# A recurrent layer and a mixture of experts on one core: three transpositions go from TensorE to the DMA queue of SyncE

## What is computed

```python
def cell(h, x):                       # 256 steps, one after the other; D = 512
    gi, gh = x @ W_ih + b_ih, h @ W_hh + b_hh
    r = sigmoid(gi_r + gh_r); z = sigmoid(gi_z + gh_z)
    n = tanh(gi_n + r * gh_n)
    return (1 - z) * n + z * h
...
scores = einsum('btd,ed->bte', h, Wg)            # E = 8
probs  = softmax(top 2 of scores)
y = sum over the two experts e:  prob_e * ((silu(h @ W1[e].T) * (h @ W2[e].T)) @ W3[e].T)
out = x + y
```

## Time and profile before

| | |
|---|---|
| median of 3 runs | 1501.19 us |
| span of the profiled execution | 1501.1 us, 88729 instructions |
| time of the profiled execution outside its span | about 0.1 us, by the median of the runs |
| busy: PE, PEld | 1409.4 us (94%), 1227.2 us (82%) |
| busy: DVE, ACT, POOL | 1043.8 (70%), 896.3 (60%), 415.8 (28%) |
| ACT copies out of tr_ps and gn_bank | 56.3 (L845), 52.6 (L853), 9.0 and 10.0 (L856), 32.0 us (L863) |
| granted TensorE clock, mean | 0.976 |
| steps 52 to 255 of the recurrence | about 296 to 1356 us |
| the 20 tiles behind it | from about 1357 us |

### The profile page before, as it was taken

One profiled execution on the slowest core, in us unless ns is written; L12 is line 12 of the kernel. 1 busy time (PEld: TensorE's weight loads), 2 busy tenths in 40 slices (PEclk: granted clock), 3 DMA queues, 4 the chain that ended last, 5 costly groups with the idle time before them and its releaser, 6 DMA issues.

```text
span 1501.1 us, 88729 instructions
## 1 busy us (share of the span) xinstructions
PE 1409.4 (94%) x37804; PEld 1227.2 (82%) x37804; DVE 1043.8 (70%) x4116; ACT 896.3 (60%) x2319; POOL 415.8 (28%) x850
## 2 busy tenths in 40 slices
PE   2888878899999999999999999999999999998997
PEld 1888778888888888888888888888888888885664
DVE  7788887777677677777777767776777776764333
ACT  6677675555565556655556555665556655555664
POOL 1011112123322232222332223222333222326443
PEclk9999887899999999999999999999999999999999
DMA  8445413112221222212222122211222212223431
GB/s 290 124 130 140 134 45 90 40 32 40 46 39 39 46 46 40 39 39 46 40 46 40 39 46 46 41 38 40 46 40 46 40 39 47 39 40 79 60 49 16
DMA packets 99011, 88.64 MB, mean 59 GB/s; under 512 B 41407, under 2 KB 74175, under 8 KB 98624
## 3 DMA queue, kind: packets, MB, share of 16 engines
q0 software_dynamic: 17952, 33.64, 12.9%
q1 hardware_dynamic: 80672, 49.32, 11.5%
HBM read 59.12 MB, written 35.72 MB: 63 GB/s over the span
## 4 chain that ended last, share of the span: by engine, by line
PE 83%; DVE 10%; issue 3%; ACT 1%; POOL 1%; DMA 1%; SPq 0%; DVEq 0%; POOLq 0%; ACTq 0%
PE gn_bank L1366 12%; PE gz_ps L1366 12%; PE y_ps L1458 9%; PE b_ps L1388 9%; PE a_ps L1422 8%; PE b_ps L1422 8%; PE gi_ps L1388 8%; PE gr_ps L1357 6%; PE gr_ps L1351 6%; DVE wexp L1037 2%; PE tr_ps L1436 2%; PE tr_ps L1446 2%; PE tr_ps L1478 1%; DVE npre L1067 1%; DVE nmh L1073 1%
## 5 line engine op out<-in xcount | busy, mean ns | idle before, releaser
L1366 PE MATMUL gz_ps<-hlog,whh 128*128 128x32 f16 x8192 | 246.0, 177 | 6.1 <-issue 6.0
L1366 PE MATMUL gn_bank<-hlog,whh 128*128 128x32 f16 x8192 | 245.2, 177 | 2.4 <-issue 2.2
L625 POOL DMA_INDIRECT out_y<-work,mt x57 | 93.9, 1648 | 546.2 <-PE gz_ps L1366 309.6
L1366 PEld LDWEIGHTS gz_ps<-hlog,whh 128*128 128x128 f16 x8192 | 224.1, 96 | 6.9 <-issue 6.7
L1366 PEld LDWEIGHTS gn_bank<-hlog,whh 128*128 128x128 f16 x8192 | 224.2, 96 | 2.7 <-issue 2.7
L1351 PEld LDWEIGHTS gr_ps<-hlog,whh 128*128 128x128 f16 x4096 | 130.6, 96 | 53.9 <-DVE hlog L1080 32.4
L1351 PE MATMUL gr_ps<-hlog,whh 128*128 128x16 f16 x4096 | 141.9, 170 | 31.3 <-DVE hlog L1080 28.3
L1388 PE MATMUL b_ps<-xs,wih 128*128 128x64 f16 x4752 | 162.3, 197 | 3.4 <-issue 2.1
L1458 PE MATMUL y_ps<-wexp,work 128*128 x639 | 159.0, 382 | 1.9 <-ACT work L845 1.9
L1388 PEld LDWEIGHTS b_ps<-xs,wih 128*128 128x128 f16 x4752 | 153.3, 101 | 5.1 <-issue 3.5
L810 ACT ACTIVATE rs<-rpre,sc 128x64 f32<-128x64 f32 x256 | 88.0, 344 | 112.7 <-DVE rpre L1054 112.5
(11 more groups left out here) (217 smaller groups left out, 2550.3 us busy)
## 6 DMA issues: line engine op xcount, KB each, us to landing
wexp<-in_w_units SPq DMA_DIRECT2D x46, 256.0 KB, 3.8
x_raw<-in_x_feat SPq DMA_DIRECT2D x32, 256.0 KB, 3.7
out_y<-in_x_tok SPq DMA_DIRECT2D x16, 512.0 KB
h_tok<-xrow SPq DMA_DIRECT2D x32, 256.0 KB, 2.0
wexp<-in_w_hh SPq DMA_DIRECT2D x4, 768.0 KB, 6.8
wexp<-in_w_inproj SPq DMA_DIRECT2D x4, 768.0 KB, 11.8
wexp<-in_w_units SPq DMA_DIRECT2D x15, 192.0 KB, 4.5
mt<-meta SPq DMA_DIRECT2D x71, 1.0 KB, 1.7
```

Source lines behind the costliest of these rows:

```text
L625: pool.indirect_dma_start(out=out, out_offset=bass.IndirectOffsetOnAxis(ap=mt[:, j % RING, 0:1].bitcast(I32), axis=0), in_=ysc[y_slot(j)], ...
L1366: mm = pe.matmul(dst[:, j], whh[:, i, k, m * P:(m + 1) * P], h[:, k], start=False, stop=True, skip_group_check=True)
```

## The change

The three turnings leave TensorE and ScalarE. SyncE issues a DMA transposition for each instead, from SBUF to SBUF: turn_gathered (xg to xT), turn_hidden (hid16 to hidT) and turn_rows (hlog to xrow). Each waits for what it reads and for its target to be free. The blocks T and X and the bank tr_ps are gone; R1 keeps the score product (scores). The semaphores gathered_turned, hid_turned and rows_turned take the place of tr_mm, tr_taken, x_mm and x_taken. VectorE gets a wait for rows_turned at every eighth step, before it writes over a group in hlog. In xT the blocks of 128 features lie in another order, which A and B follow (2 * k + a).

```diff
         j, s = divmod(t - FIRST, CYCLE)
         if j >= 0:
-            before = [("T", j - 1)], [("D0", j - 1)], [("D1", j - 1)], []
+            before = [], [("D0", j - 1)], [("D1", j - 1)], []
             work += ([("A", j)], [("B", j)], [], [])[s] + (before[s] if j else [])
...
-        if (t + 1 - FIRST) % CYCLE == 0 and t + 1 >= FIRST:
-            work += [("X", (t + 1 - FIRST) // CYCLE)]
...
-            tail += [("E", j + 1), ("X", j + 1)]
+            tail += [("E", j + 1)]
...
-        if j - 1 < TILES:
-            tail += [("T", j - 1)]
...
-        tr_ps = ps("tr_ps", [P, 1024], F16)
...
+            def turn_gathered(j):
+
+                sp.wait_ge(x_gathered[j % 4], 16 * (j // 4 + 1))
+                if j:
+                    sp.wait_ge(b_mm, j if j <= MAIN_TILES else j - 1)
+                sp.dma_start_transpose(xT[x_slot(j)], xg[g_slot(j)]).then_inc(gathered_turned[j % 2], 16)
+
+            def turn_hidden(j):
+
+                sp.wait_ge(ffn_ops, ffn(j, "HID_LO"))
+                if j:
+                    sp.wait_ge(d_mm, j)
+                sp.dma_start_transpose(hidT, hid16[:].rearrange("p i n -> p (i n)")).then_inc(hid_turned, 16)
+
+            def turn_rows(g):
+
+                sp.wait_ge(gru_ops, gru(GS * g + GS - 1, "H_LO"))
+                if g:
+                    sp.wait_ge(h_stored, 16 * g)
+                sp.wait_ge(x_mag, min(g + 3, UNITS_X))
+                sp.dma_start_transpose(xrow[:].rearrange("p (c f) -> p c f", f=P),
+                                       hlog[:, g % 2].rearrange("p k i t -> p (k i t)")).then_inc(rows_turned, 16)
+
             def store_rows(g):
-                sp.wait_ge(tr_taken, TR_NO["R1", g] + 1)
+                sp.wait_ge(rows_turned, 16 * (g + 1))
                 sp.dma_start(h_tok[g * P:(g + 1) * P], xrow[:]).then_inc(h_stored, 16)
 
             load_x(0)
...
+                if t % GS == 1 and t >= GS:
+                    turn_rows(t // GS - 1)
...
-                    store_rows(LAST)
-                take_up(j)
+                    elif t == base(j) - 2:
+                        turn_gathered(j)
+                    elif t == base(j) + 3:
+                        turn_hidden(j)
+
+            turn_rows(LAST)
+            take_up(MAIN_TILES + 2)
+            for j in range(MAIN_TILES + 1, TILES):
+                turn_gathered(j)
+                if j - 2 >= MAIN_TILES:
+                    turn_hidden(j - 2)
+                if j + 2 < TILES:
+                    if stage(j + 2) == LAST and stage(j + 1) < LAST:
+                        store_rows(LAST)
+                    take_up(j + 2)
+            turn_hidden(TILES - 2)
+            turn_hidden(TILES - 1)
 
         @block.gpsimd
         def _(pool):
@@ -604,11 +633,11 @@
                 there = min(stage(j), LAST) + 1
...
-                    pool.wait_ge(x_mm, j - 3 - MAIN_TILES)
+                    pool.wait_ge(gathered_turned[(j - 3) % 2], 16 * ((j - 3) // 2 + 1))
                 elif j > MAIN_TILES:
                     pool.wait_ge(gi_mm, GI_BATCHES)
                 elif j:
-                    pool.wait_ge(tr_mm, TR_NO["X", j - 1] + 1)
+                    pool.wait_ge(gathered_turned[(j - 1) % 2], 16 * ((j - 1) // 2 + 1))
...
-                    act.wait_ge(tr_mm, TR_NO["T", j - 1] + 1)
+                    act.wait_ge(hid_turned, 16 * j)
                 S.activation(hid16[:, 0, 0:HE], hid[:], ACT.Copy, scale=hscale[:, 0:1]).then_inc(hid_hi, 1)
-
-            def take_turned(j):
-                act.wait_ge(tr_mm, TR_NO["T", j] + 1)
-                if j:
-                    act.wait_ge(d_mm, j)
-                S.copy(hidT[:].rearrange("p c t -> p (c t)"), tr_ps[:, 0:2 * HB * P]).then_inc(tr_taken, 1)
-
...
+                if t % GS == 0 and t >= 2 * GS:
+                    dve.wait_ge(rows_turned, 16 * (t // GS - 1))
...
-                    if j <= MAIN_TILES:
-                        pe.wait_ge(tr_taken, TR_NO["X", j] + 1)
-                    else:
-                        pe.wait_ge(x_taken, j - MAIN_TILES)
+                    pe.wait_ge(gathered_turned[j % 2], 16 * (j // 2 + 1))
...
-                        mm = pe.matmul(dst, xT[x_slot(j)][:, a * K + k], part[:, k],
+                        mm = pe.matmul(dst, xT[x_slot(j)][:, 2 * k + a], part[:, k],
...
-                    pe.wait_ge(tr_taken, TR_NO["T", j] + 1)
+                    pe.wait_ge(hid_turned, 16 * (j + 1))
...
-            def turn_rows(g):
-
-                if TR_NO["R1", g]:
-                    pe.wait_ge(tr_taken, TR_NO["R1", g])
+            def scores(g):
+
```

More of the change, by code:

```diff
@@ L154, in gru_moe_kernel @@
             tail += [("B", j)]
-        if j - 1 < TILES:
-            tail += [("T", j - 1)]
-    TR_NO = {b: n for n, b in enumerate([b for b in main + tail if b[0] in ("T", "R1")
-                                              or b[0] == "X" and b[1] <= MAIN_TILES])}
     ROUTED_BEFORE_A, BATCH_BEFORE_B, B_BEFORE_BATCH = {}, {}, {}
@@ L412, in gru_moe_kernel @@
         tanh_n = sem("tanh_n")
-        tr_mm = sem("tr_mm")
-        tr_taken = sem("tr_taken")
+        rows_turned = sem("rows_turned")
         score_mm = sem("score_mm")
@@ L425, in gru_moe_kernel @@
         x_gathered = [sem(f"x_gathered_{i}") for i in range(4)]
-        x_mm = sem("x_mm")
-        x_taken = sem("x_taken")
+        gathered_turned = [sem(f"gathered_turned_{i}") for i in range(2)]
         a_mm = sem("a_mm")
@@ L433, in gru_moe_kernel @@
         hid_hi = sem("hid_hi")
+        hid_turned = sem("hid_turned")
         ffn_ops = sem("ffn_ops")
@@ L585, in _ @@
                             take_up(j + 1)
-            for j in range(MAIN_TILES + 2, TILES):
-                if stage(j) == LAST and stage(j - 1) < LAST:
-                    store_rows(LAST)
-                take_up(j)
+                    elif t == base(j) - 2:
[14 more added lines that the diff above has]
+            turn_hidden(TILES - 1)
         @block.gpsimd
@@ L921, in _ @@
                             take_y(j - 1)
-                if t >= GS and t % GS == (3 if t < BS * EARLY else 2):
-                    take_rows(t // GS - 1)
                 if t >= GS and t % GS == (4 if t < BS * EARLY else 3):
                     probabilities(t // GS - 1)
-                if t >= FIRST - 1 and s == CYCLE - 1:
-                    take_x(j + 1)
                 if t % GS == 6 and t // GS + 2 < UNITS_X:
@@ L1421, in up @@
                     for k in range(K):
-                        mm = pe.matmul(dst, xT[x_slot(j)][:, a * K + k], part[:, k],
+                        mm = pe.matmul(dst, xT[x_slot(j)][:, 2 * k + a], part[:, k],
                                        start=(i == 0 and k == 0), stop=(i == 2 and k == K - 1))
                 mm.then_inc((a_mm, b_mm)[w], 1)
-            def turn_x(j):
-                pe.wait_ge(x_gathered[j % 4], 16 * (j // 4 + 1))
-                dst = tr_ps[:]
-                if j > MAIN_TILES:
-                    dst = gn_bank[:].bitcast(F16)
-                    if j - 1 > MAIN_TILES:
-                        pe.wait_ge(x_taken, j - 1 - MAIN_TILES)
-                elif TR_NO["X", j]:
-                    pe.wait_ge(tr_taken, TR_NO["X", j])
-                for c in range(2 * K):
-                    mm = pe.transpose(dst[:, c * P:(c + 1) * P], xg[g_slot(j)][:, c * P:(c + 1) * P], ident[:])
-                mm.then_inc(tr_mm if j <= MAIN_TILES else x_mm, 1)
-            def turn_hidden(j):
-                pe.wait_ge(ffn_ops, ffn(j, "HID_LO"))
-                if TR_NO["T", j]:
-                    pe.wait_ge(tr_taken, TR_NO["T", j])
-                for i in range(2):
-                    for b in range(HB):
-                        at = (i * HB + b) * P
-                        mm = pe.transpose(tr_ps[:, at:at + P], hid16[:, i, b * P:(b + 1) * P], ident[:])
-                mm.then_inc(tr_mm, 1)
             DOWN = [(i, b) for i in range(3) for b in range(HB)]
@@ L1474, in turn_rows @@
                 h = hlog[:, g % 2]
-                for i in range(2):
-                    for k in range(K):
-                        at = (i * K + k) * P
-                        mm = pe.transpose(tr_ps[:, at:at + P], h[:, k, i], ident[:])
-                mm.then_inc(tr_mm, 1)
                 for i in range(2):
@@ L1529, in run @@
                     up(n, 1)
-                elif kind == "T":
-                    turn_hidden(n)
-                elif kind == "X":
-                    turn_x(n)
                 elif kind == "D0":
@@ L1538, in run @@
                 elif kind == "R1":
-                    turn_rows(n)
+                    scores(n)
                 elif kind == "R2":
```

21 lines of the change are left out of this document (removed).

## The result

Four runs of the changed kernel have a median of 1483.62 us (1479.41 to 1487.69), four of the kernel before 1501.69. The ratio is 0.988 [0.986, 0.991]. It is 1.2% faster, but the time lies just outside the range. The profiled run took 1481.52 us, its span 1479.8.

A forecast was written before the change was run, and what follows sets the result against it. The prediction took TensorE, 83% of the chain of waits, to bound the kernel. 53.9 us less in the loop, 2.1 added where the recurrence ends and 10.1 less behind it gave 61.9 less: 1439.3 us, range 1426 to 1482.

The forecast's parts named there:

- What goes: In the recurrence loop, TensorE's turnings of gathered rows, hidden activations and h disappear: 53.9 us less.
- Beside the recurrence these are hidden ... Added there: 0: During the recurrence the DMA transpositions land before anyone needs them, with 7.8 us of room or more: 0 us added.
- The junction: Where the recurrence ends, SyncE's queue delays the fetch of mt and the gathers, so A of 55 starts later: 2.1 us added.
- TensorE stays the bound by 0.2 us: Tiles behind the recurrence: TensorE's 5.52 us a tile, instead of 6.31, stays just above the other loops' 5.3.
- two loops of 5.3 us: Behind the recurrence, the hidT buffer's loop and SyncE's queue order could limit a tile, each at 5.3 us.
- the first loop: Behind the recurrence, one hidT buffer: D, then the next hidden transposition: 1.94 + 3.2 + 0.2 = 5.3 us a tile.
- the second: Behind the recurrence, SyncE's queue order over two tiles: 1.0 + 2.0 + 3.7 + 1.8 + 1.9 + 0.2 = 10.6 us, 5.3 a tile.
- slow tail: Rival: hidden transpositions take 5.2 us, gathered 6.0, so tiles behind the recurrence take 7.35 us; total 1473; chance 0.14.
- The end: Pipeline emptying after the last tiles: 12.5 us from A of 70 until D of 70 starts, instead of 10.7.
- Block by block: Rival: each 128-column block costs a small DMA's 1.7 us, 13.6 per gathered transposition; about 2250; chance 0.12 including otherwise above 6.7.
- The Trainium skill's 261 GB/s: DMA transpose rate giving an estimated 2.7 us for 256 KB with the 1.7 us floor; total then about 1437.
- The recurrence did not become the limit: Judges the rival that the step of A can't shrink below 4.78 us, so 17 us stay: 1456; chance 0.05.

The follow-up runs named there:

- the first set: Runs of the changed kernel and the kernel before, together on a chip not on record: ratio 0.988 [0.986, 0.991].
- the third set: Later runs on chip 6, both kernels profiled again beside two variants: changed kernel against kernel before 1.003 [1.001, 1.006].
- loop_gh: Against the changed kernel, all rows of h and everything behind the recurrence turned by TensorE again: ratio 0.993 [0.991, 0.996] to the kernel before.
- plain_copies: Changed kernel with every DMA transposition replaced by a plain DMA copy of the same tile, nothing turned: ratio 0.970 [0.968, 0.972] to the kernel before.

## Why the prediction was wrong

**What goes: right.** 48.2 us forecast between steps 56 and 248, 48.4 in the undisturbed steps.

**"Beside the recurrence these are hidden ... Added there: 0": wrong in the early part.** As a wait it held: TensorE waits for no transposition before the recurrence ends. But I counted only who waits for the transfers, and not what they share engines with. Next to the 512 KB copies they come with a late instruction fetch: +6.9 instead of -3.6 us in the first set, +3.6 in the third; loop_gh shows that this is not the only way to a late fetch. In steps 56 to 248 another 7 us of stalls came, with plain copies as well; 3 of them show as longer idle times behind instruction fetches, and the cause of the rest is open. That the stalls would stay as they were was an assumption I never wrote down.

**The junction: mis-sized, as far as one pair of traces can tell.** A of 55 starts 4.8 us later behind the last step than before (40.4 and 35.6), forecast 2.1. In the third set it is only 1.3 (41.3 and 40.0), for there the kernel before takes 4.4 us more, with the granted clock at its lower level for 10 us instead of 3. In the first set's trace mt lands 0.9 later than before (by the medians) and the gathered transposition of tile 54 is waited for:

```profile
1348.23 3.15 PE L1415 MATMUL a_ps<-wexp,wih 128*128 x12 [3.10 <-DMA wih<-wih]
```

**"TensorE stays the bound by 0.2 us": the step that failed.** Two windows of 15 tiles (A of 55 to A of 70), the columns stretch, length, PE, PEld, DVE, ACT, POOL busy, granted clock, DMA share, GB/s; first before, then after:

```profile
1387.70:1482.30 94.60, 94.60 (x709) 60.17 (x707) 37.30 (x106) 58.55 (x105) 37.93 (x28) 1.00 0.32 46
```
```profile
1356.10:1454.40 98.30, 85.56 (x495) 48.30 (x496) 36.91 (x105) 35.22 (x75) 39.23 (x29) 1.00 0.74 119
```

TensorE's work fell by 9.0 us, and 12.7 of idle time came: 6.55 us a tile instead of 5.52, 98.3 instead of 82.8. I had two loops of 5.3 us under a bound of 5.52. In this window the median hidden transposition takes 3.7 us, not 3.2, so the first loop is 1.94 + 3.7 + 0.2 = 5.8 us. From the issue of a hidden transposition to that of the next gathered one SyncE takes 3.9 (median of 14), not 1.0 + 2.0, so the second is (3.9 + 3.6 + 1.8 + 1.9 + 0.2) / 2 = 5.7. At their medians both loops are already over TensorE's 5.52, and single transfers take up to 5.8, as the DMA share went from 0.32 to 0.74; that this spread makes up the rest, from 5.8 to 6.55, I read from tiles like the one below and have not shown for each. One tile of it:

```profile
1408.74 1.37 SPq L544 DMA_TRANSPOSE wih<-wih  x1
...
1414.82 1.96 PE L1415 MATMUL a_ps<-wexp,wih 128*128 x12 [2.30 <-DMA wih<-wih]
...
1417.36 2.11 PE L1428 MATMUL y_ps<-wexp,work 128*128 x9 [0.58 <-issue]
...
1419.55 1.21 SPq L551 DMA_TRANSPOSE work<-hid  x1
...
1424.93 2.11 PE L1428 MATMUL y_ps<-wexp,work 128*128 x9 [1.88 <-DMA work<-hid]
```

The gathered transposition took about 6 us, the hidden one waited for D of the tile before (to 1419.5) and then took 5.4: the loop is 2.1 + 5.4 = 7.5 us for such a tile. This is the rival "slow tail" (5.2 and 6.0 us, 7.35 a tile, 1473) in part of the tiles, and I gave it 0.14.

**The end: a term left out.** A of 70 to D of 70 was 12.5 us, as forecast. But from D of 70 to the end it is 12.8 us, not 8.0, for the scatter-adds came out:

```profile
1466.47 1.56 POOL L654 DMA_INDIRECT out_y<-work,mt  x1 [3.69 <-DMA out_y<-wih,mt]
...
1471.89 1.56 POOL L654 DMA_INDIRECT out_y<-wih,mt  x1 [3.86 <-DMA out_y<-work,mt]
1475.43 1.56 POOL L654 DMA_INDIRECT out_y<-wih,mt  x1 [1.98 <-DMA out_y<-wih,mt]
```

Junction 2.7, tiles 15.5, end 4.8: the 23 us missed behind the recurrence.

**The other rivals.** Block by block is out: eight blocks land in 4.6 us. The Trainium skill's 261 GB/s (DMA: Bandwidth & Descriptors, "Latency and other measured facts") had given an estimated 2.7 us for 256 KB; the median here is 4.6 beside the recurrence and 3.6 behind it, the fastest of all 3.0, so the measurement decides for less than that rate. The recurrence did not become the limit: a step of A shrank to 4.43.

## What to carry to other kernels

Take work off an engine by DMA only where the transfer has room for twice its usual time; in a stage whose other loops stand within a few tenths of the engine's own, a transfer's median over the whole program says little; its median and spread in that stage, beside the other traffic, do. List every loop there, the scatter-adds' too, before you shorten a tile. And price a transfer that nobody waits for by what it shares engines with, the instruction fetch above all. Measure in more than one set of runs: the same kernel was 1.2% and 1.4% faster in two sets here and 0.3% slower in a third.

## What was not expected of the hardware

- A transposition of 128 rows by 768 f16 columns holds SyncE's queue 1.21 us (median of the trace after), one of 1024 columns 1.26, one of h 1.58; the longest took 3.2. A plain DMA of the same tiles (plain_copies) holds it 0.47 to 0.53.
- TensorE stood 4.03 us for a 16 KB instruction fetch while a transposition ran beside a 512 KB copy from DRAM to DRAM; without the one or the other the early part is 268.9 to 277.6 us instead of 277.7 to 287.3, with one exception, loop_gh (282.8).
- In two sets of runs, with the kernel before much the same in its loop (1002.3 and 999.4 us), the same kernel with transpositions took 961.0 and 976.2 us in steps 56 to 248. Sets with such gaps and sets without came on one and the same chip.
